# Window attention block on one core: maxima from pairs of heads, with operand rings of their own

## The reference

```python
xn = _layernorm(xw, ln_g, ln_b)                       # per token, 96 channels
q, k, v = (xn @ qkv_w.T + qkv_b) split into 12 heads
attn = softmax(einsum('bhnd,bhmd->bhnm', q * SCALE, k) + bias)
seq = shortcut + (attn @ v) @ proj_w.T + proj_b
seq2 = batchnorm(depthwise_conv3x3(seq))
h = gelu(seq2 @ w1.T + b1)
out = seq2 + (h @ w2.T + b2)
```

## Time and profile before

| | |
|---|---|
| median of 3 runs | 3153.03 us (3148.52 to 3162.89) |
| profiled execution | 3152.75 us, its span 3151.0 us |
| PE busy | 3029.5 us (96%) |
| DVE busy | 2893.3 us (92%) |
| ACT busy | 2777.0 us (88%) |
| GpSimd busy | 1958.7 us (62%) |
| mean granted TensorE clock | 0.995 |
| DMA | 288.31 MB, mean 92 GB/s |

### The profile page before, as it was taken

One profiled execution on the slowest core, in us unless ns is written; L12 is line 12 of the kernel. 1 busy time (PEld: TensorE's weight loads), 2 busy tenths in 40 slices (PEclk: granted clock), 3 DMA queues, 4 the chain that ended last, 5 costly groups with the idle time before them and its releaser, 6 DMA issues.

```text
span 3151.0 us, 199775 instructions
## 1 busy us (share of the span) xinstructions
PE 3029.5 (96%) x88076; PEld 2108.1 (67%) x88076; DVE 2893.3 (92%) x4901; ACT 2777.0 (88%) x4869; POOL 1958.7 (62%) x2578
## 2 busy tenths in 40 slices
PE   5999999999999999999999999999999999999997
PEld 3666666666766666666666666766666666666664
DVE  5899999999999999999999999999999999999996
ACT  4799999998988999989898998998988999898986
POOL 3566666666666666666666666666666666666665
PEclk9999999999999999999999999999999999999998
DMA  2233333333333333333333333333333333333331
GB/s 65 82 97 92 96 95 91 97 93 94 94 92 96 91 98 90 96 90 95 96 91 96 91 96 94 93 96 91 96 91 93 93 95 94 93 97 92 95 92 43
DMA packets 269922, 288.31 MB, mean 92 GB/s; under 512 B 55651, under 2 KB 252580, under 8 KB 269062
## 3 DMA queue, kind: packets, MB, share of 16 engines
q1 hardware_dynamic: 235364, 198.14, 22.8%
q0 software_dynamic: 32768, 77.14, 7.0%
q10 hardware_dynamic: 930, 0.26, 0.0%
HBM read 39.34 MB, written 38.54 MB: 25 GB/s over the span
## 4 chain that ended last, share of the span: by engine, by line
PE 93%; issue 3%; ACT 1%; DVE 1%; SPq 1%; DMA 1%; POOL 1%; POOLq 0%; ACTq 0%; DVEq 0%
PE d_ps L271 22%; PE st_ps L315 12%; PE o_ps L361 11%; PE sm_ps L336 10%; PE b_ps L379 7%; PE b_ps L415 7%; PE a_ps L271 4%; PE b_ps L271 4%; PE a_ps L282 3%; PE a_ps L283 3%; PE a_ps L284 3%; PE d_ps L282 1%; PE b_ps L283 1%; PE d_ps L284 1%; PE d_ps L283 1%
## 5 line engine op out<-in xcount | busy, mean ns | idle before, releaser
L790 DVE SCALAR_TENSOR_TENSOR s<-ximg,cols,s 96x392 f32<-96x392 f32 x1792 | 1142.3, 637 | 30.7 <-POOL s L656 3.2
L764 DVE TENSOR_REDUCE mx<-sm_ps 128x12 f16<-128x588 f32 x1024 | 784.9, 767 | 131.6 <-PE sm_ps L336 128.8
L496 ACT ACTIVATE p<-st_ps 128x588 f32<-128x588 f32 x1024 | 672.4, 657 | 186.6 <-PE st_ps L315 183.5
L666 POOL DMA_DIRECT2D ox<-o_sb x1024 | 582.8, 572 | 28.5 <-ACT o_sb L521 14.9
L336 PEld LDWEIGHTS sm_ps<-k_all,q_all 127*49 127x49 f16 x24576 | 459.7, 103 | 172.3 <-issue 76.9
L271 PE MATMUL d_ps<-g,w_s 128*64 128x392 f32 x3072 | 558.3, 499 | 0.2 <-issue 0.2
L639 POOL TENSOR_TENSOR s<-ximg,cols 96x392 f32<-96x392 f32 x256 | 216.0, 844 | 524.4 <-DVE y L827 523.6
L315 PEld LDWEIGHTS st_ps<-q_all,k_all 128*49 128x49 f16 x24576 | 436.3, 103 | 157.8 <-issue 107.3
L315 PE MATMUL st_ps<-q_all,k_all 128*49 128x49 f16 x24576 | 517.3, 186 | 21.7 <-issue 19.5
L336 PE MATMUL sm_ps<-k_all,q_all 127*49 127x49 f16 x24576 | 508.1, 185 | 27.7 <-issue 17.9
L628 POOL TENSOR_TENSOR xl<-xn,xh 96x392 f16<-96x392 f32 x256 | 258.9, 1011 | 262.1 <-ACT xh L577 244.7
(11 more groups left out here) (126 smaller groups left out, 5959.3 us busy)
## 6 DMA issues: line engine op xcount, KB each, us to landing
ox<-o_sb POOLq DMA_DIRECT2D x1024, 73.5 KB
k_all<-kh SPq DMA_DIRECT2D x512, 75.0 KB
q_all<-qh SPq DMA_DIRECT2D x512, 75.0 KB
x_sb<-in_x SPq DMA_DIRECT2D x256, 147.0 KB, 2.4
out<-y SPq DMA_DIRECT2D x256, 147.0 KB
q_all<-ql SPq DMA_DIRECT2D x256, 75.0 KB
k_all<-kl SPq DMA_DIRECT2D x256, 75.0 KB
q_all<-mxt SPq DMA_DIRECT2D x256, 9.4 KB, 2.1
```

The source lines that it names most:

```text
L496: af(p32[:, p, :, :].rearrange("p (b h) n -> p b h n", b=2), st_ps[:, :, 0:HALF].rearrange("p b (h n) -> p b h n", n=TOK), ACT.Exp).then_i ...
L666: nc.gpsimd.dma_start(ox[:, c % 2, x4, :], o_sb[x4::4, c % 2, :, :]).then_inc(o_in[c % 2], 16)
L764: v.tensor_reduce(mx[:, c % 2, 0:HEADS, p].rearrange("p (b h) -> p b h", b=2), sm_ps[:, :, 0:HALF].rearrange("p b (h n) -> p b h n", n=TOK ...
L790: v.scalar_tensor_tensor(acc, image_rows(c, k // 3, k % 3), cw_c[:, k:k + 1], acc, ALU.mult, ALU.add)\
```

## The change

Maxima are taken from scores of the high parts alone: q high times k high plus the high part of the bias. For this there are new rings k_pair and q_pair of 114 partitions (8 rows of each of two heads, 49 bias rows of each) and 2 slots, filled by four DMAs a chunk of 37.5 KB each. In k_pair the columns of head b are zero in the rows of the other head, so one matmul of 98 columns gives the scores of two heads. A group of `max_scores` has 12 matmuls, not 24. k_all and q_all go from 4 slots to 3. `second` accumulates in a_ps, in the order 1, 0, 2. The order of the calls in the step changes on every engine.

```diff
+RING = 3
+HEAD_RING = 2
+HEAD_PAIRS = HEADS // 2
+PAIR_ROWS = 2 * HD + 2 * TOK
...
-        k_all = sb("k_all", [ROWS, 4, HEADS, NW * KP], F16)
-        q_all = sb("q_all", [ROWS, 4, HEADS, NW * KP], F16)
+        k_all = sb("k_all", [ROWS, RING, HEADS, NW * KP], F16)
+        q_all = sb("q_all", [ROWS, RING, HEADS, NW * KP], F16)
+        k_pair = sb("k_pair", [PAIR_ROWS, HEAD_RING, HEAD_PAIRS, 2, NW * KP], F16)
+        q_pair = sb("q_pair", [PAIR_ROWS, HEAD_RING, HEAD_PAIRS, NW * KP], F16)
...
+        for b in range(2):
+            row = 2 * HD + b * TOK
+            tables.append((pair_bias_f[row:row + TOK, :, :], bias_q[:, b::2, :]))
+            tables.append((pair_hot_f[row:row + TOK, b, :], eye[0:TOK, 0:KP]))
...
             def first_term(t, n, part, done, c):
...
-                    wait(sp, sm_done[3], c - 4)
-                    wait(sp, st_done[3], c - 4)
+                    wait(sp, st_done[3], c - RING)
...
+            def claim_pairs(c):
...
+                wait(sp, sm_done[3], c - HEAD_RING)
+
+            def key_heads(b, c):
...
+                wait(sp, kh_done, c)
+                sp.dma_start(k_pair[b * HD:b * HD + HD, c % HEAD_RING, :, b, :], kh[b:C:2, c % 2, :]).then_inc(pair_in[c % HEAD_RING], 16)
+
+            def query_heads(b, c):
...
+                wait(sp, qh_done, c)
+                sp.dma_start(q_pair[b * HD:b * HD + HD, c % HEAD_RING, :, :], qh[b:C:2, c % 2, :]).then_inc(pair_in[c % HEAD_RING], 16)
...
             for s in range(STEPS):
+                term(k_all, 0, kh, kh_done, s - 4)
+                store(s - 11)
                 load(s)
-                first_term(k_all, 0, kh, kh_done, s - 3)
+                claim_pairs(s - 3)
+                key_heads(1, s - 3)
+                key_heads(0, s - 3)
+                query_heads(1, s - 3)
+                query_heads(0, s - 3)
+                first_term(k_all, 1, kl, kl_done, s - 3)
+                term(q_all, 1, qh, qh_done, s - 3)
+                maximum_row(s - 4)
+                term(q_all, 2, ql, ql_done, s - 3)
                 term(k_all, 2, kh, kh_done, s - 3)
                 term(q_all, 0, qh, qh_done, s - 3)
-                term(q_all, 2, ql, ql_done, s - 3)
-                term(k_all, 1, kl, kl_done, s - 3)
-                term(q_all, 1, qh, qh_done, s - 3)
-                store(s - 11)
-                maximum_row(s - 4)
...
             def max_scores(c, p):
...
-                    wait_ring(pe, exp_in, c, 6 * 16)
+                    wait_ring(pe, pair_in, c, 4 * 16)
...
-                for h in range(HEADS):
+                for g in range(HEAD_PAIRS):
                     for w in range(2):
-                        n, c0 = (2 * p + w) * KP, h % HH * TOK
-                        last = mm(sm_ps[64 * w:64 * w + TOK, h // HH, c0:c0 + TOK], q_all[0:MAXROW, r, h, n:n + TOK],
-                                  k_all[0:MAXROW, r, h, n:n + TOK], start=True, stop=True)
+                        n, c0 = (2 * p + w) * KP, 2 * g % HH * TOK
+                        last = mm(sm_ps[64 * w:64 * w + TOK, 2 * g // HH, c0:c0 + 2 * TOK].rearrange("p (b t) -> p b t", t=TOK),
+                                  q_pair[:, r, g, n:n + TOK], k_pair[:, r, g, :, n:n + TOK], start=True, stop=True)
...
-                halves(d_ps[0:128, 0:CT], w2_s[:, k, :], g[:, k, :], start=k == 0, stop=k == 2).then_inc(s_done[k], 1)
+                halves(a_ps[0:128, 0:CT], w2_s[:, k, :], g[:, k, :], start=k == 1, stop=k == 2).then_inc(s_done[k], 1)
```

More of the change, by code:

```diff
@@ L438, in second @@
                 wait(pe, g_done[k], c)
-                if k == 0:
-                    free(pe, (g_done[0], c), (xn_done, c+7), (y_done, c-1))
-                halves(d_ps[0:128, 0:CT], w2_s[:, k, :], g[:, k, :], start=k == 0, stop=k == 2).then_inc(s_done[k], 1)
+                if k == 1:
+                    free(pe, (g_done[1], c), (v32_done, c+5), (ql_done, c+6), (y_done, c-1))
+                halves(a_ps[0:128, 0:CT], w2_s[:, k, :], g[:, k, :], start=k == 1, stop=k == 2).then_inc(s_done[k], 1)
             for s in range(STEPS):
+                second(s - 9, 2)
+                exp_scores(s - 4, 0)
+                max_scores(s - 3, 2)
+                keys(s - 2)
+                queries(s - 2)
+                exp_scores(s - 4, 1)
+                values_times_p(s - 5, 3)
+                values_times_p(s - 5, 2)
+                variance(s - 1)
+                values(s - 3)
+                max_scores(s - 3, 3)
                 exp_scores(s - 4, 2)
-                max_scores(s - 3, 3)
                 projection(s - 6)
+                values_times_p(s - 4, 1)
+                values_times_p(s - 4, 0)
+                hidden(s - 8, 1)
                 hidden(s - 8, 0)
                 maxima_rows(s - 3)
-                hidden(s - 8, 1)
                 hidden(s - 8, 2)
+                max_scores(s - 2, 0)
+                second(s - 8, 1)
+                second(s - 8, 0)
                 exp_scores(s - 4, 3)
-                max_scores(s - 2, 0)
-                second(s - 8, 0)
-                second(s - 8, 1)
-                second(s - 8, 2)
-                keys(s - 1)
                 max_scores(s - 2, 1)
-                queries(s - 1)
-                exp_scores(s - 3, 0)
                 centred(s)
-                max_scores(s - 2, 2)
-                exp_scores(s - 3, 1)
-                values_times_p(s - 4, 2)
-                values_times_p(s - 4, 3)
-                variance(s)
-                values(s - 2)
-                values_times_p(s - 3, 0)
-                values_times_p(s - 3, 1)
         @block.scalar
@@ L484, in _ @@
             act.wait_ge(tables_made, 1)
-            for r in (2, 3):
-                dst, src = query_slot(r)
-                af(dst, src, ACT.Identity).then_inc(slot_ready[r], 1)
+            for dst, src in (key_pair_slot(1, 0), key_pair_slot(1, 1), query_pair_slot(1)):
+                af(dst, src, ACT.Identity).then_inc(pair_ready[1], 1)
             act.wait_ge(ready, 4)
@@ L517, in outputs @@
                     return
-                wait(act, pv_done[1 if half == 0 else 3], c)
+                wait(act, pv_done[0 if half == 0 else 2], c)
                 if half == 0:
@@ L579, in _ @@
             for s in range(STEPS):
+                if real(s - 8):
+                    act.preload_act_table_set("gelu_and_others")
+                gelu(s - 8, 1)
+                gelu(s - 8, 0)
+                input_high(s - 1)
                 gelu(s - 8, 2)
@@ L724, in _ @@
                 v.tensor_copy(*slot(0)).then_inc(slot_ready[0], 1)
+            for dst, src in (key_pair_slot(0, 0), key_pair_slot(0, 1), query_pair_slot(0)):
+                v.tensor_copy(dst, src).then_inc(pair_ready[0], 1)
             dve.wait_ge(loaded, 16 * LOADS)
@@ L815, in values_out @@
                 wait(dve, v_done, c)
-                wait(dve, pv_done[3], c - 2)
+                wait(dve, pv_done[2], c - 2)
                 v.tensor_tensor(v32[:, c % 2, :, :, :].rearrange("p h n (d x) -> p (h n d) x", x=4)[:, :, 0:2],
@@ L826, in block_out @@
                 dve.wait_ge(stored[c % 2], (c // 2 + 1) * 16)
-                v.scalar_tensor_tensor(y[0:C, c % 2, :], d_ps[0:C, 0:CT], b2_c, s2[0:C, c % 2, :], ALU.add, ALU.add)\
+                v.scalar_tensor_tensor(y[0:C, c % 2, :], a_ps[0:C, 0:CT], b2_c, s2[0:C, c % 2, :], ALU.add, ALU.add)\
                  .then_inc(y_done, 1)
@@ L851, in _ @@
             for s in range(STEPS):
-                maxima(s - 2, 2)
+                query_low(s - 1)
+                tap(s - 7, 8)
+                normalise(s - 5)
                 values_out(s - 2)
+                maxima(s - 2, 3)
                 input_normal(s)
-                maxima(s - 2, 3)
                 image_sum(s - 5)
```

100 lines of the change are left out of this document (61 added, 39 removed).

## The result

The changed kernel takes 3103.56 us (median of four runs, 3097.09 to 3104.88) where the kernel before takes 3157.96 in the same comparison: a ratio of 0.9825 with an interval of 0.9804 to 0.9846, 1.75% faster. The profiled execution took 3104.88 us with a span of 3103.1, 28 us above the forecast of 3077 and inside the range.

What follows compares the result with a forecast made beforehand. The prediction took PE to bound the kernel, with other engines close behind. Its terms took a step from 11.95 to 11.63 us; 3152.75 - 255 x 0.32 + 6 gave 3077 us, range 3020 to 3158.

Steps and rivals of the forecast that it cites:

- (d): New waits of PE in the new order, tight at y, kl and ql: +0.20 us a step, bounds 0 and 0.6.
- (a): Four max_scores groups on PE, 12 matmuls of 98 columns each, 0.26 us for 0.32: -0.24 us a step.
- (b): second on PE cut into 8 and 4 matmuls, accumulating in a_ps: 2.03 us against 2.00, +0.03 a step.
- (c): PE running out of instructions: fewer matmuls and dense groups standing apart cut it by 0.31 us a step.
- (f): GpSimd's changed order, with the four DMA issues moved ahead: y and taps give the same waits, cost 0.
- (g): Ends of the run, mainly setup with more table DMAs and DVE copies: +6 us, range 0 to +12.
- rival of pairs that don't overlap: Wide max_scores pairs on PE take 0.52 us a group, +0.80 a step, total 3342 us; chance 0.03.
- (e): SP queue with the added head copies: at most 8.7 of 11.6 us a step, price 0.
- waits eat much: Rival: PE's new waits cost 0.42 us a step, a step 11.85, total 3133 us; chance 0.12.
- Starvation stays: Rival: instructions reach PE late for another reason than density; a step 11.94, total 3156 us; chance 0.08.
- The mark that I had set, PE below 95% of the span: Sign that the forecast is wrong: PE's share below 95% means the bound has moved to DVE's order.
- The mark for (c): Sign that PE's instruction shortage is cured: no idle "issue" inside groups, and its chain share below 1%.

Runs made afterwards that it cites:

- experiment 5: Changed kernel with max_scores written as 24 matmuls of 49 columns again, new orders kept: 3194.94 us, ratio 1.0071 to the kernel before.
- experiment 1: Changed kernel with first_product put ahead of second_product on GpSimd (the swapped kernel): 3059.67 us, ratio 0.9651 to the kernel before; run again 3061.33.
- experiment 7: Kernel before with two more SP copies a chunk, of kh and qh into an unread scratch tile: 3311.76 us, ratio 1.0477.
- experiments 4: Changed kernel with all engines' orders set back to before: 3192.5 us, ratio 1.0068; the same but SP keeping the new order: 3180.83 us, 1.0022.
- 6: Kernel before with the projection moved on PE into the dense stretch, between values_times_p and exp_scores: 3301.83 us, ratio 1.0408.

## Why the prediction was nearly right

The forecast step was 11.63 us, the measured one 11.74; 0.11 x 255 = 28 us is the whole gap to 3077. It splits by the floor, the stalls and the rest (the measured (d) is what remains of the step when floor and stalls are taken off):

| | forecast | measured |
|---|---|---|
| (a) + (b), floor of a step | -0.21 | 11.35 - 11.54 = -0.19 |
| (c) starvation | -0.31 | -0.29 |
| (d) new waits, with (f) | +0.20 | +0.27 |
| (g) ends | +6 us | +5.6 us |

That the sum came so near is partly luck. (f) stood at 0 and measured 0.18, (d) without it stood at 0.20 and measured about 0.1, and the two errors nearly cancel; the places where (d) expected PE to wait were not those where it waited.

- **(a) Maxima**: right. The distance between starts is 0.265 us where a group of the same shape follows and 0.286 at the two behind a group of another shape, for 0.322 before. Six pairs of 98 columns run at 0.044 us, 0.45 ns a column, as the pairs of keys did. The Trainium skill, "TensorE: Matmul & The Clock Gate", section "Back-to-back issue gap", has about 81 ns a matmul for 128 columns; the estimate by it was 0.97 us a group. The trace disagrees: 12 take 0.265, 22 ns each. The rival of pairs that don't overlap fell with it.
- **(b)** `second` in two parts costs 1.329 + 0.661 = 1.99 us, not 2.03. There is one change of shape more (the projection, 0.83 where it was 0.74), at the upper end of what I had allowed. Centring came out 0.02 shorter, and is back at 0.69 with the narrow matmuls of experiment 5 ahead of it. Two `exp_scores` took 0.34 before, behind a group of another shape, and none stands so now. Variance counts 0.03 less, where it starts behind a wait. In all the floor fell by 0.19 for a forecast of 0.21.
- **(c) Starvation**: the size was right, and so was the density of the stretch as the handle. The reason was half of it. The term named both, fewer matmuls and groups that stand apart, and laid the cure on the second; experiment 5 shows that without the 12 matmuls fewer in each of four groups two thirds of the stalls return. The changed kernel has no block eaten in under 3.3 us, and 18 of 554 stall; before, 123 of the 209 blocks eaten in under 3.1 us did.
- **(d) New waits**: the step that failed, together with (f), though its size missed by only 0.07. I laid the tight places out from usual durations, and found kl without slack and ql late by 0.09. PE hardly waits for them (1.1 and 1.3 us in all). It waits for y, for which I had 0.12 us of slack: the layout was right there, and the tap ahead of y (two DVE instructions before it, in 103 of 110 steps) was not 0.61 us long. The distance from the group before queries exceeds its floor by 37 us in 97 steps, and that before variance by 11 us in 108; 48 us over the 231 steps counted are 0.21 of the 0.27.
- **(f) GpSimd order**, "y and taps give it the same waits. 0", is the term that was mis-sized. It looked at what GpSimd waits for, and not at what runs beside it. `second_product` ahead of `first_product` has no wait for y, starts right behind `input_low`, and holds up a tap in 47% of the steps. It costs 0.176 us a step, 45 us, as experiment 1 measured. With it at zero the step is 11.56, and my sum 11.63 would have been 0.07 too high: (d) proper is then about 0.1, half of what I took.
- **(e) SP queue**: right in its price. 5.6 us in 4 waits of PE for q_pair, where I had written none.
- **(g) Ends**: right in sum. Setup made 4.5 of it (first centring at 27.83, before 23.34), but not as I had it: the wait for half_c, behind the four table transfers, grew by 3.3 us (16.4 for 13.1), where I had 1, and the copies cost less.

Of the rivals, "waits eat much" came nearest. "Starvation stays" fell, and experiment 7 makes its strongest reason, traffic, unlikely. The mark that I had set, PE below 95% of the span, did not show what it was meant to: PE is at 97%, and yet 15% of the chain is DVE. The mark for (c), "issue" below 1% of the chain, misled the other way: it is 5%, though the stalls are 9.6 us, and 1% in experiment 1. Busy time of PE's records doesn't fall when a group is drawn out by short waits; the chain's shares do move.

## What to carry to other kernels

When an order is changed, list for each moved instruction not only what it waits for but which instruction of the neighbouring engine it will now run beside; where GpSimd reads SBUF and the DVE instruction takes two inputs from it, let the later one sit out the rest of the other engine's run, and see whether a wait hangs on it. When an engine runs short of instructions, change both their number and how closely the short ones stand together: here either alone gave nothing. And a buffer given to a second user turns an uncritical result into an urgent one: read its producer's slack again with the longest duration in the trace, not with the usual one.

## What the runs showed of the hardware

- A tap on DVE with two SBUF inputs takes 0.61 us alone. Where it starts 0.33 us before the end of a GpSimd instruction it ends 0.43 us after it (0.75 us, experiment 1), and when GpSimd starts another one right behind, 0.43 us after that one (1.55 us). Starting 0.17 us before the end costs the tap nothing; then GpSimd pays, 1.18 us for 0.84. `first_product`, which starts behind y and behind the next tap, takes 1.09 us in the changed and in the swapped kernel, for 0.84 before the change. DVE instructions with one SBUF and one PSUM input (kl, xn) take 0.55 us beside GpSimd as without.
- PE's waits for instructions lie at one place modulo 256 of its instruction count: with the lower threshold 24 of 25 after the change and 121 of 143 before, the others one instruction on. PE goes on some 1.4 us after the end of the last packet of its instruction queue. In the kernel before a block eaten in less than about 3.1 us stalled more often than not (123 of 209), longer ones seldom; experiments 4 (66 stalls behind slower blocks) and 6 (fast blocks mostly without one) show that this length alone doesn't decide. "Runtime: NRT & Kernel Launch" of the Trainium skill, section "Instruction fetch mechanics", calls this cost mostly hidden; in these traces it was 76 us before the change and 116 in one of the experiments.
- A change on PE between column halves or quarters and another layout costs 0.09 us each time (`exp_scores` 0.41 for 0.32, the projection 0.83 for 0.74), and pairs on column halves run at 0.45 ns a column down to 98 columns (0.265 us for six pairs).
